# Graph layer on one core: edge counts built in chunks of two units of 125 edges in place of four

## What is computed

```python
e = leaky_relu(as_n[src] + ad_n[dst], 0.2)
p = exp(e - segment_max(e, dst)[dst])
s = segment_sum(p, dst)
out = segment_sum((p / s[dst])[:, :, None] * h[src], dst) + b
```

## Time and profile before

| | us |
|---|---|
| median of 3 runs | 1558.21 (1556.44 to 1563.09) |
| profiled execution, its own time | 1557.13 |
| its span | 1555.0 |
| TensorE busy in the span | 1419.0 (91%) |
| VectorE busy in the span | 1066.4 (69%) |
| mean granted TensorE clock | 0.95 |

### The profile page before, as it was taken

How to read it: one execution, slowest core, us unless ns; L and a number is a source line. 1 busy time by engine, 2 the same in 40 slices (tenths; PEclk the granted TensorE clock), 3 DMA queues, 4 the chain that set the end, 5 groups by cost and what they waited for, 6 DMA issues and landing times.

```text
span 1555.0 us, 21194 instructions
## 1 busy us (share of the span) xinstructions
PE 1419.0 (91%) x8222; PEld 1315.6 (85%) x8222; DVE 1066.4 (69%) x1950; ACT 468.6 (30%) x780; POOL 36.5 (2%) x41
## 2 busy tenths in 40 slices
PE   5999898999999697787999999999999999998788
PEld 4985566988888597687999999999999999997663
DVE  6857988788888642157677677767767766776645
ACT  3210122233333420133433343243333334322231
POOL 2100000000000021000000000000000000000000
PEclk9989999999999898788999999999999999999985
DMA  8220000222111184500010110101012010004003
GB/s 243 97 82 0 2 1 1 81 81 81 64 65 50 57 260 152 134 31 33 29 41 1 64 51 18 64 34 36 1 64 69 1 64 34 6 17 130 1 0 99
DMA packets 23300, 90.99 MB, mean 59 GB/s; under 512 B 3549, under 2 KB 4800, under 8 KB 20269
## 3 DMA queue, kind: packets, MB, share of 16 engines
q1 hardware_dynamic: 22289, 87.47, 17.4%
q10 hardware_dynamic: 924, 2.30, 0.5%
HBM read 78.70 MB, written 11.06 MB: 58 GB/s over the span
## 4 chain that ended last, share of the span: by engine, by line
PE 50%; DVE 8%; ACT 3%; issue 1%; DVEq 0%
PE psum L1470 21%; PE psum L101 8%; PE psum L102 8%; PE psum L103 8%; DVE prob L1198 2%; PE psum L1553 2%; DVE prob L1192 2%; DVE hN L1212 1%; ACT prob L1346 1%; PE psum L1484 1%; DVE x1l L1218 1%; PE psum L1521 1%; ACT x1h L1352 0%; DVE acc L1233 0%; DVE xll L1224 0%
## 5 line engine op out<-in xcount | busy, mean ns | idle before, releaser
L1470 PE MATMUL psum<-hN,prob 125*125 125x193 f32 x2400 | 412.9, 328 | 10.8 <-DVE hN L1212 7.6
L1470 PEld LDWEIGHTS psum<-hN,prob 125*125 125x125 f32 x2400 | 398.1, 189 | 12.4 <-issue 9.3
L1346 ACT ACTIVATE prob<-prob,acol 125x1250 f32<-125x1250 f32 x120 | 160.9, 1341 | 396.7 <-DVE prob L1192 396.7
L1198 DVE SCALAR_TENSOR_TENSOR prob<-prob,cnt 125x1250 f32<-125x1250 f32 x120 | 174.8, 1457 | 80.2 <-ACT prob L1346 80.2
L1192 DVE SCALAR_TENSOR_TENSOR prob<-vrow,ncol,urow 125x1250 f32<-125x1250 f32 x120 | 181.9, 1516 | 0.0
L689 DVE CUSTOM_DVE_ANT_0 junk<-mask,arow 125x1250 bf16<-125x1250 uint8 x120 | 174.8, 1457 | 3.1
L101 PE MATMUL psum<-wph,x1h 128*125 128x384 f32 x360 | 135.6, 377 | 26.8 <-DVE x1l L1218 26.8
L101 PE MATMUL psum<-woh,xlh 128*125 128x384 f32 x360 | 127.9, 355 | 15.7 <-DVE acc L1233 15.7
L102 PE MATMUL psum<-wpl,x1h 128*125 128x384 f32 x360 | 128.7, 357 | 0.0
L103 PE MATMUL psum<-wph,x1l 128*125 128x384 f32 x360 | 128.2, 356 | 0.0
L102 PE MATMUL psum<-wol,xlh 128*125 128x384 f32 x360 | 123.3, 343 | 0.0
(11 more groups left out here) (199 smaller groups left out, 2200.9 us busy)
## 6 DMA issues: line engine op xcount, KB each, us to landing
arow<-scratch_a SPq DMA_DIRECT2D x12, 625.0 KB, 4.1
urow<-scratch_uv SPq DMA_DIRECT2D x12, 625.0 KB, 4.1
vrow<-scratch_uv SPq DMA_DIRECT2D x12, 625.0 KB, 5.7
wq_raw<-in_w_qkv SPq DMA_DIRECT2D x6, 1152.0 KB, 7.3
wp_raw<-in_w_pair SPq DMA_DIRECT2D x6, 1152.0 KB, 7.2
wo_raw<-in_w_out SPq DMA_DIRECT2D x6, 1152.0 KB, 5.8
wl<-in_w_gat SPq DMA_DIRECT2D x4, 1152.0 KB, 6.5
xN<-in_x SPq DMA_DIRECT2D x10, 336.0 KB
```

The lines of the kernel that those rows point to most:

```text
L1198: nc.vector.scalar_tensor_tensor(prob[n % RING][:, :], prob[n % RING][:, :], 1.0, cnt[:, n % NT, :], op0=ALU.min, op1=ALU.mult).then_inc(p ...
L1346: nc.scalar.activation(prob[n % RING][:, :], prob[n % RING][:, :], ACT.Exp, bias=acol[:, n // NT, n % NT:n % NT + 1]).then_inc(e_ready, 1)
L1470: last = nc.tensor.matmul(bank(t // 2)[0:P, 193 * (t % 2):193 * (t % 2) + 193], ring[:, t * P:(t + 1) * P], hN[i % 2][:, j, 193 * s:193 * ...
```

## The change

`CE`, the number of units in a chunk and of places in the rings, goes from 4 to 2. `CHUNKS` (160 units by `CE`) goes from 40 to 80 with it, and all shapes that are written with the two names follow: `chunk_i` and `chunk_f` are 80 x 250 in place of 40 x 500, `ends` 80 x 2, `ends_bc` 10 x 80 x 2, and the input `dst_c` is cut in the same way. No other line changes.

```diff
 E = 20000
 ET = E // P
-CE = 4
+CE = 2
 CHUNKS = ET // CE
```

## The result

The changed kernel takes 1584.78 us (median of four runs, 1582.60 to 1590.53) against 1560.22 for the kernel before in the same comparison, 24.6 us more. The comparison's own ratio of the runs is 1.0179, with a 95% interval of 1.0152 to 1.0207; the quotient of the two medians is 1.0157. The forecast was 1587.5 us against 1558.2, 29.3 us more, a ratio of 1.0188. The profiled execution took 1584.86 us with a span of 1582.8, 27.8 us over the span of before.

What follows compares the result with a forecast made beforehand. VectorE bounds the count stage inside windows; with two places the two lags (1.67 us a pair) would. Stage +30.1 less 0.65 at the front gives +29.5 on 1557.1, 1586.6; median forecast 1587.5 us, 8-in-10 range 1579 to 1602.

Steps and rivals of the forecast that it cites:

- the two lags: Count stage's rings: 0.76 us from write to weight load, 0.91 from there to the next write; 1.67 us a pair.
- Units: Count stage's loops: 178 units in place of 196; at 0.617 us each, 18 fewer would save 11.1 us.
- The sum of the stage: Count stage, first to last weight load: 138.1 + 32.7 + 0.9 = 171.7 us against 141.56, 30.1 more.
- 0.9 for the clock: After window 0, at the lower clock: two pairs at 2.1 us in place of 1.67 add 0.9 us.
- Between windows: Gaps between the stage's windows, untouched: 3.49 us eight times and 4.81 after window 0, in all 32.7.
- Loop edges at nothing: 89 loop ends in place of 49 on both engines cost nothing; upper bound 18 us.
- Finding the reach: Reduces and cast of `ends` at the kernel's front: shorter, saving 0.65 us at most, at least nothing.
- The later stages: Everything behind the count stage: unchanged but for a shift in time.
- The ring of two is enough: Rival, count stage: places return within 1.23 us, VectorE keeps its pace, kernel faster at 1546.5 us; chance 0.05.
- The clock falls: Rival, count stage: TensorE's lower share drops the clock, 1626 us, or 1607 if half the time; chance 0.08.
- The loop edges are exposed: Rival, count stage's loop ends: the pair grows by up to 0.2 us, to 1605 us; chance 0.06.
- The reach isn't finer: Rival, count stage: still 196 units, nine pairs more at 1.67 us, 1602.5 us; chance 0.01.

Runs made afterwards that it cites:

- e5: Kernel before with two places for `hot_src`, `hot_dst` keeping four and written ahead of the wait (196 units): 1589.92 us, ratio 1.0209.
- e9: Kernel before with four places, but `hot_free` starting at 2, so VectorE may lead by two units: 1601.90 us, one run.
- e6: Kernel before with two-unit chunks (178 units), four fixed places in the loop body and a tail for odd windows: 1547.66 us, ratio 0.9941.
- e1: Kernel before with two places in each ring, chunks still of four units (196 units, 49 loop ends): 1602.97 us, ratio 1.0305.
- e7: e6 with two places in place of four and no padding after the tail (178 units, 41 loop ends): 1590.42 us, ratio 1.0212.
- e8: Kernel before with four places, but `hot_free` starting at 3, so VectorE may lead by three units: 1567.78 us, ratio 1.0047.
- e4: Kernel before (196 units) looping over half chunks, 98 loop ends, four places addressed by a flipping register: 1606.75 us, ratio 1.0326.
- e3: Changed kernel with one place in each ring in place of two (178 units): 1827.61 us, one run.
- e2: Changed kernel's two-unit chunks (178 units, 89 loop ends) with four places addressed by a flipping register: 1593.51 us, ratio 1.0231.

## Why the prediction was right

**Which engine bounds the stage, and the two lags.** Right, and the core of the result. 0.76 and 0.91 us were read from the kernel before, where they lay hidden under a lead of four, and the changed kernel shows them to the hundredth in window 0. The doubt that something in 0.91 was the wake of a long wait is gone: it is the same at a wait of 0.34 us. e5 shows that the chain made of them sets the pace, e9 that the lead and not the memory does.

**Units.** 178, as counted. e6 shows what they are worth without the ring: 9.9 us of stage, 9.5 us by the medians. It was right to book the gain of 11.1 as lost: while VectorE waits for TensorE, its units are not what one pays for.

**The sum of the stage.** 171.7 forecast, 173.58 measured. The pairs in window 0 are right: 167.69 - 125.29 = 42.40 us by the rows against 25 x 1.67 + 0.62 = 42.37. The 1.9 us that were missing lie after window 0, first where I had 4.81 us between the windows and 0.9 for the clock. The weight loads there, and the windows view:

```profile
167.69 0.37 PEld L581 LDWEIGHTS psum<-hot_src,hot_dst 125*125 125x125 bf16 x3 [0.25 <-DVE hot_src L424]
...
172.93 1.67 PEld L581 LDWEIGHTS psum<-hot_src,hot_dst 125*125 125x125 bf16 x6 [4.28 <-DVE hot_src L424]
...
175.16 0.64 PEld L581 LDWEIGHTS psum<-hot_src,hot_dst 125*125 125x125 bf16 x3 [0.55 <-DVE hot_src L424]
...
177.38 0.58 PEld L581 LDWEIGHTS psum<-hot_src,hot_dst 125*125 125x125 bf16 x3 [0.55 <-DVE hot_src L424]
...
179.26 0.37 PEld L581 LDWEIGHTS psum<-hot_src,hot_dst 125*125 125x125 bf16 x3 [0.47 <-DVE hot_src L424]
```

```profile
171.10:177.70 6.60, 4.76 (x13) 2.52 (x14) 3.50 (x11) 0.00 (x0) 0.00 (x0) 0.50 0.07 10
```

The first comes 172.93 - 167.69 = 5.24 us after the last of window 0, and three pairs (2.23, 2.22, 1.88) instead of two are slow, 1.3 us in all: the clock is at 0.50 for 6.6 us and more, where the kernel before had 3.2. The length of this stretch differs from run to run (e1, e5 and e7 have the short one, e9 the long one, all with a lead of two), so I take it for chance. The last step of window 1 is 0.81 in place of 0.62. The eight other gaps sum to 28.4 where I had 27.9. And window 7 takes 9.26 us where the sum has 8.97: its pairs take 1.73 us, since the lag from `hot_dst` to the weight load is 0.83 there (270.47 to 271.30) and not 0.76. Why it is longer in that one window stays open. Together these are 1.8 of the 1.9 us.

**Between windows.** Right: 3.50 to 3.67 us, as before.

**Loop edges at nothing.** Right for the changed kernel: e7 halves them and the stage stays within 0.6 us. But e8 shows the cover to be thinner than I wrote: at a lead of three 0.09 us an edge come out in window 0. In the changed kernel's window 0 they don't: 25 pairs take what the two lags give. My upper bound was also miscounted: four branches of 56 ns at 89 edges are 20 us, and 18 only at 79 pairs.

**Finding the reach, 0.65 us.** The work saved was right, and what it was worth was not. The two reduces take 0.41 us each in place of 0.67 and the cast 0.28 in place of 0.41, and VectorE's next layer norm begins at 18.66 in place of 19.26, 0.60 us earlier. But TensorE's wait of 4.00 us ends no earlier. VectorE and GpSimd (POOL) in the kernel before, then in the changed kernel:

```profile
19.96 1.80 POOL L310 TENSOR_TENSOR wah_low<-wah_raw,wah_high 128x768 fp32r<-128x768 f32 x1 [14.60 <-ACT wah_high L444]
...
21.48 0.70 DVE L344 TENSOR_SCALAR xN<-xN,moments,rstd 125x768 f32<-125x768 f32 x1
```

```profile
20.00 1.81 POOL L310 TENSOR_TENSOR wah_low<-wah_raw,wah_high 128x768 fp32r<-128x768 f32 x1 [14.60 <-ACT wah_high L444]
...
20.88 1.34 DVE L344 TENSOR_SCALAR xN<-xN,moments,rstd 125x768 f32<-125x768 f32 x1
...
22.28 1.12 PEld L506 LDWEIGHTS psum<-ident,xN 125*128 125x128 f32 x6 [4.00 <-DVE xN L344]
```

The write of `xN` starts 0.60 us earlier, takes 1.34 us in place of 0.70, and ends at 22.22 in place of 22.18. In both kernels that is 0.4 us after the end of the GpSimd pass (21.81 and 21.76). All five kernels with 80 chunks show the 1.34 and all six with 40 chunks the 0.70, each time with an end 0.4 us after GpSimd's. That VectorE's write is held up by GpSimd's pass is my reading of these ends; no run here takes the pass away. What is shown is that the 0.65 us come to nothing at TensorE.

**The later stages.** Forecast as unchanged; they took 4.4 us less (stage and start +32.2, span +27.8). It is not this change: the span behind the last unit is 1288.4 us before and 1283.9 in the changed kernel, but with the chunks of before it is also 1288.6 (e1) and 1281.8 (e4), and with those of the changed kernel 1287.4 (e7) and 1288.0 (e6). In large part it is the granted clock, which swings in the stage of the earlier trace rows. Behind the last unit the clock is at the lower level for 138.5 us before and for 131.8 in the changed kernel, and over the eleven profiles this time goes with the length of that span, from 123 us (e4, 1281.8) to 163 us (e3, 1296.3). The same stretch of the kernel before and of the changed kernel by window:

```profile
550.00:700.00 150.00, 122.16 (x593) 117.81 (x592) 49.61 (x52) 28.22 (x33) 18.55 (x15) 0.85 0.47 138
```

```profile
583.00:733.00 150.00, 123.17 (x617) 119.38 (x616) 52.34 (x54) 30.37 (x35) 18.46 (x15) 0.87 0.47 137
```

0.85 and 0.87 of 150 us: 3 us of full clock more, as I take it by chance of how its swings fall. So the agreement of the total is in part luck. The profiled execution took 1584.86 us against the 1586.6 forecast for it: 1.9 us more from the stage, 0.9 more from the reach, 4.4 less from behind the stage. The forecast for the median, 1587.5, should by its own terms (1586.6 + 1.1) have been 1587.7; and the kernel before, at 1558.2 in the forecast, measured 1560.2 in the comparison, so the step by medians is 24.6 us where 29.3 was forecast.

**The rivals.** None came true. "The ring of two is enough" is refuted by the pace and by e1. "The clock falls" is refuted for two places: in the changed kernel 1.00 throughout window 0. The Trainium skill (TensorE: Matmul & The Clock Gate, section A second HAM failure mode: psum-queue depth-cycling) had spoken for it; with two places the clock of the changed kernel falls once in the stage, after window 0, as it does in the kernel before, and no run with two places shows a swing from pair to pair. With one place e3 does show the clock falling and coming back, seven times in 404 us. "The loop edges are exposed" is refuted by e7; the Trainium skill's 108 ns for a compare-and-branch (Advanced Engine Details and Errata, section Control Flow Timing) is the median on neither engine; in the changed kernel the medians are 56 ns (VectorE, line 417 above) and 213 ns (TensorE, line 576, 76 to 340). "The reach isn't finer" is refuted by the 178.

## What to carry to other kernels

A ring between two engines needs a lead of (lag from write to use + lag from use to release) / (the bounding engine's time for a unit), rounded up, to keep the pace; here 1.67 / 0.617 = 2.7, so three. A place beyond that can still pay, since VectorE may then be one unit further ahead when each window starts: the fourth was worth up to 10.7 us of stage here, some 6 us of it for this reason and about 1 us for loop edges. Both lags can be read in the profile of the kernel with the deeper ring, but in one window of ten they were not what window 0 showed. When one constant sets two things (here the grain of the loop's bounds and the depth of the ring), take them apart before judging either: the grain gains 10 us, the depth costs 41. Before a ring is addressed by a register, look at what the sequencer of the waiting engine then has to do for each unit: here that, with the loop's end that it leaves exposed, cost as much as the lost places.

## What the hardware showed unasked

With fixed places the next unit's weight load starts 0.05 us after `hot_src` ends (140.36 + 0.54 against 140.95 in the changed kernel). With three computed operand addresses a unit it starts 1.76 us after (141.45 to 143.21 in e2), and the stage runs at 1.67 us a pair, 0.84 us a unit, for matmuls that take 0.52. That the engine's sequencer is the bound is read from the `issue` in these rows and from VectorE's waiting and the matmuls' 0.52 us, which rule out the other two.

With one place, where the two engines wait for each other at every unit, TensorE was at its lower clock for most of the stage (e3), while the shorter waits of the changed kernel leave it at 1.00 in window 0. The step between them is 2.23 us against 0.84 a unit, so one place costs far more than twice what two cost: 272.7 us of stage against 41.3, both over e6.

A write by VectorE of 125 x 768 elements took 1.34 us in place of 0.70 when it began while a GpSimd pass had 0.9 us to run, and in all eleven kernels, with the early start or the late one, it ended 0.4 us after that pass: work taken off VectorE ahead of it bought nothing.
